# Two multi-head attentions whose first projections are made one stage earlier

## What is computed

```python
def multi_head(x, ctx, Wq, Wk, Wv, Wo, key_bias, bq, bk, bv, bo):   # x is normed
    q, k, v = heads(x @ Wq + bq), heads(ctx @ Wk + bk), heads(ctx @ Wv + bv)
    scores = einsum('bhqd,bhkd->bhqk', q, k) / 4 + key_bias[:, None, None, :]
    return merge(einsum('bhqk,bhkd->bhqd', softmax(scores), v)) @ Wo + bo
# layer 1 has key_bias and no bq, bk, bv, bo; layer 3 has these and no key_bias
x = x + tanh(g_xattn[n]) * attention_n(layernorm(x), ctx)
x = x + tanh(g_ffn[n]) * feed_forward_n(layernorm(x))
```

## Time and profile before

| | |
|---|---|
| median of three executions | 1390.92 us |
| the profiled execution: its own time, its span | 1390.4 us, 1388.7 us |
| busy in the span: PE, DVE, POOL, ACT | 1041.1 (75%), 803.3 (58%), 597.8 (43%), 561.4 us (40%) |
| mean granted TensorE clock | 0.859 of 2.4 GHz |
| combine of layer 0, first PE instruction to the next block's | 320.13 to 404.75 us |
| norm block ahead of layer 3, first DVE instruction to the next block's PE | 1094.85 to 1111.79 us |

### The profile page before, as it was taken

The page is one execution under the profiler, slowest core; times in us unless marked ns, Lnnn a source line. Parts: engine busy times, 40 slices in busy tenths (PEclk is TensorE's granted clock), DMA queues, the critical chain, the costliest instruction groups (busy, mean ns, idle before and its releaser), DMA issues. The chain is left out here.

```text
span 1388.7 us, 26577 instructions
## 1 busy us (share of the span) xinstructions
PE 1041.1 (75%) x8492; PEld 774.3 (56%) x8493; DVE 803.3 (58%) x1763; ACT 561.4 (40%) x1319; POOL 597.8 (43%) x746
## 2 busy tenths in 40 slices
PE   5777378884558888740799916798887689997998
PEld 3666167883336666630699912455555367776443
DVE  4666154442655877865455545455554538775876
ACT  2462023431126566533334305556552247774000
POOL 1473605565235667657000062556652247763000
PEclk9986589996669999955899966889898789997999
DMA  3463218862041111147777521000000100000000
GB/s 106 119 183 113 87 43 309 289 234 86 29 163 30 36 34 35 35 130 239 254 252 257 193 69 54 1 1 1 0 1 8 39 8 20 16 17 5 16 23 23
DMA packets 70682, 123.47 MB, mean 89 GB/s; under 512 B 15481, under 2 KB 41859, under 8 KB 70595
## 3 DMA queue, kind: packets, MB, share of 16 engines
q1 hardware_dynamic: 63011, 101.64, 22.5%
q0 software_dynamic: 7584, 20.72, 4.4%
HBM read 52.98 MB, written 24.64 MB: 56 GB/s over the span
## 5 line engine op out<-in xcount | busy, mean ns | idle before, releaser
L303 ACT ACTIVATE xnT<-bank 128x256 f32<-128x256 f32 (+1 forms) x112 | 42.2, 381 | 90.7 <-PE bank L292 89.4
L2411 PE MATMUL bank<-l0f_x_high,l_weights 128*128 128x256 bf16 x256 | 51.7, 320 | 34.0 <-issue 20.8
L2820 POOL DMA_DIRECT2D l_results<-keep x23 | 12.5, 544 | 135.3 <-DVE keep L2923 135.3
L3182 PE MATMUL bank<-l_weights,room 128*128 x552 | 65.1, 273 | 4.3 <-DVE room L3210 2.8
L3170 PE MATMUL bank<-room,xnT 128*128 128x128 bf16 x1104 | 67.1, 222 | 0.0
L3170 PEld LDWEIGHTS bank<-room,xnT 128*128 128x128 bf16 x1104 | 65.3, 99 | 0.3
L882 PE MATMUL bank<-ident,l_weights 128*77 128x128 f32 x256 | 39.7, 298 | 33.0 <-DVE l_weights L1073 28.3
L2243 DVE SCALAR_TENSOR_TENSOR l3f_total<-bank,l3f_share,l3f_total 128x256 f32<-128x256 f32 x112 | 54.2, 484 | 15.6 <-PE bank L2161 11.6
L2626 PE MATMUL bank<-room,l0r_placed 128*128 128x128 bf16 x936 | 61.5, 224 | 0.0
L1783 POOL TENSOR_TENSOR l2x_probs<-l2x_probs,l2x_inverse 128x333 f32<-128x333 f32 x64 | 49.5, 796 | 25.4 <-DVE l2x_inverse L1688 25.4
L3182 PEld LDWEIGHTS bank<-l_weights,room 128*128 128x128 bf16 x552 | 52.7, 98 | 12.3 <-issue 5.4
(11 more groups left out here) (430 smaller groups left out, 3252.0 us busy)
## 6 DMA issues: line engine op xcount, KB each, us to landing
xnT<-l_weights SPq DMA_DIRECT2D x23, 1024.0 KB, 5.0
l0r_placed<-l_weights SPq DMA_DIRECT2D x39, 512.0 KB, 3.6
room<-in_L_ffn_weights SPq DMA_DIRECT2D x20, 512.0 KB, 5.0
l0w_staging<-in_L_ffn_weights SPq DMA_DIRECT2D x16, 480.0 KB, 3.8
l_weights<-in_L_ffn_weights SPq DMA_DIRECT2D x16, 384.0 KB, 3.1
room<-l_rows SPq DMA_DIRECT2D x39, 128.0 KB, 3.1
l_results<-room POOLq DMA_DIRECT2D x39, 128.0 KB, 3.1
l_rows<-l_weights SPq DMA_DIRECT2D x16, 184.0 KB, 2.2
```

What stands on the lines that cost most here:

```text
L303: act.activation(self.chip.xnT[:, :, span(t, P)], bank[:, 0:DIM].rearrange("p (k n) -> p k n", k=KD), ACT.Copy).then_inc(self.copied, 1)
L2411: last = pe.matmul(self.bank[:, c, branch * width:(branch + 1) * width], self.weights[w][:, at:at + P], x[:, s, k, :], start=(i == 1), sto ...
L3182: last = pe.matmul(bank[:, 2 + u, 0:DIM], h[:, u, c * P:(c + 1) * P], expert_part(split[:, w, :, :], e, KD * hidden_width + c * DIM, DIM), ...
```

## The change

`multi_head_loads` becomes a class `HeadsAhead`, which holds the loads, the keys and first queries (now in `chip.room`; the queries take the place of `Wk`), layer 1's bias rows, and for layer 3 the values (in `chip.keep`). Its methods are called in the block before. Keys go through banks 2 and 3, values through 4 and 5, two batches to a copy.

```diff
 class HeadsAhead(Loads):
+    def tensor_keys(self, pe, chunks=range(KD)):
+        pe.wait_ge(self.loaded, 16 * len(self.copies))
+        for m in chunks:
+            for h in range(2):
+                wait(pe, self.kT_ready, 2 * m - 1 + h)
+                ...
+    def tensor_queries(self, pe, norm):
+        pe.wait_ge(norm.copied, TPB)
+        pe.wait_ge(self.kT_ready, 2 * KD)
+        ...
+    def tensor_values(self, pe, twos):
+        for n in twos:
+            wait(pe, self.v_ready, n - 1)
+            ...
+    def vector_values(self, dve, twos):
+        for n in twos:
+            dve.wait_ge(self.v_projected, n + 1)
+            ...
 # multi_head_attention
-            project_q(0)
-            project_v(range(BATCH // 2))
+            project_v(early)       # layer 1: batches 0 to 2, layer 3: none
 ...
-            project_v(range(BATCH // 2, BATCH))
+            project_v(late)        # layer 1: batches 3 to 7, layer 3: none
 # relu_square_experts, first block, SP
+                sp.wait_ge(logits_ready, 1)
+                ahead.sync(sp)
 # relu_square_experts, last block
-                ahead.sync(sp)
-                tiles.tensor(pe)
+                ahead.tensor_keys(pe, range(1))
+                tiles.tensor(pe, range(4))
+                ahead.tensor_keys(pe, range(1, 2))
+                tiles.tensor(pe, range(4, 8))
+                ahead.tensor_values(pe, range(2))
+                tiles.tensor(pe, range(8, 12))
+                ahead.tensor_values(pe, range(2, 4))
+                ahead.tensor_queries(pe, norm)
+                tiles.tensor(pe, range(12, TILES))
 # ... DVE there, group g: moments of g, norming of g - 1, and then
+                    if g >= 2:
+                        ahead.vector_values(dve, range(2 * g - 4, 2 * g - 2) if g < tiles.groups else ())
 # combine
-            sp.wait_ge(gathered[groups - 1], 16 * per * sort.picks)
+            if not heads:
+                sp.wait_ge(gathered[groups - 1], 16 * per * sort.picks)
             ahead.sync(sp)
+            if heads:                       # DVE, ahead of group 0
+                ahead.vector_bias(dve)
+            if heads:                       # PE, ahead of its tiles; ACT likewise
+                ahead.tensor_keys(pe)
+                if g == 0 and heads:        # after group 0's tiles
+                    ahead.tensor_queries(pe, norm)
```

More of the change, by code:

```diff
@@ L785, in multi_head_attention @@
         if key_bias:
-            bias = given.bias
-            bias_parts = [st.sb(f"bias_{n}", [P, CTX], BF16) for n in ("high", "mid")]
-            bias_rows = st.sb("bias_rows", [P, CTX], BF16)
+            bias_rows = given.bias_rows
             ones = st.sb("ones", [P, P], BF16)
         else:
[L791 to L794, removed]
+            bq, bo = given.bq, given.bo
+        given.start()
+        early = range(0 if given.values_ahead else 3)
+        late = range(len(early), 0 if given.values_ahead else BATCH)
         v_projected = st.sem("v_projected")
@@ L831, in _ @@
         def _(pe):
[L832 to L838, removed]
             def project_q(b):
@@ L957, in _ @@
         def _(act):
[L958 to L963, removed]
             def copy_q(b):
-                act.wait_ge(q_projected, b + 1)
+                act.wait_ge(q_projected, b)
                 wait(act, scores_ready, GROUPS * TPB * b)
@@ L1000, in _ @@
             exponents(0, 0)
-            act.wait_ge(v_ready, BATCH)
+            if len(late):
+                act.wait_ge(v_ready, BATCH)
             act.wait_ge(ones_ready, 2)
@@ L1033, in _ @@
                 clearing.vector(dve)
+            if key_bias:
+                dve.memset(ones[:, :], 1.0).then_inc(bias_ones_ready, 1)
             dve.memset(v1[:, :, :, HEAD:HEAD + 1].rearrange("p b h d -> p (b h) d"), 1.0).then_inc(ones_ready, 1)
-            dve.wait_ge(loaded, 16 * loads)
             dve.memset(zeros[:, :], 0.0).then_inc(ones_ready, 1)
             dve.wait_ge(ones_ready, 2)
[L1038 to L1051, removed]
+            if not key_bias:
                 dve.tensor_scalar(bo[:, :], bo[:, :], chip.gate[:, gate:gate + 1], None,
-                                  ALU.mult).then_inc(bias_ready, 1)
+                                  ALU.mult).then_inc(out_bias_ready, 1)
             def copy_v(batches_of):
@@ L2095, in _ @@
             def _(dve):
-                tiles.vector(dve)
+                for g in range(tiles.groups + 1):
+                    if g < tiles.groups:
+                        norm.vector_stats(dve, *tiles.group(g))
+                    if g > 0:
+                        for t, u in tiles.group(g - 1):
+                            norm.vector_apply(dve, t, u)
+                    if g >= 2:
+                        ahead.vector_values(dve, range(2 * g - 4, 2 * g - 2) if g < tiles.groups else ())
 def nth_row(dram, i):
@@ L2939, in combine @@
         part_added = st.sem("part_added")
+        heads = isinstance(ahead, HeadsAhead)
+        if heads:
+            ahead.bias_rooms(st)
         early = 2
@@ L3010, in _ @@
                 shared.scalar(act, n, n % 2)
+            if heads:
+                ahead.scalar_keys(act)
             for g in range(groups):
@@ L3013, in _ @@
                     norm.scalar(act, t, u)
+                if g == 0 and heads:
+                    ahead.scalar_queries(act)
 def relu_experts(chip, a, weights, split_before, ahead):
@@ L3277, in attention_loads @@
     if layer < len(LAYERS):
-        return multi_head_loads(chip, a, layer)
+        return HeadsAhead(chip, a, layer)
     return Loads(chip, "none")
```

142 lines of the change are left out of this document (104 added, 38 removed).

## The result

| | changed kernel | kernel before |
|---|---|---|
| median of 19 runs each | 1394.86 us | 1388.22 us |
| lowest to highest | 1388.85 to 1398.66 | 1378.68 to 1394.15 |
| profiled execution, its span | 1390.31, 1388.6 | 1390.4, 1388.7 |
| ratio, 95% interval | 1.0052 [1.0034, 1.0071] | |

The change makes the kernel slower, by 7.2 us by the ratio, with an interval of 4.7 to 9.9 (0.3% to 0.7%). The two profiled executions hide that: the one of after is among the fastest of its 19, the one of before lies 2.2 us above its median, and their spans are 0.1 us apart. So the traces are good for stretches, not for the total.

What follows compares the result with a forecast made beforehand. It took the DVE-POOL-DVE path to bound layer 0's combine and DVE to pace the norm block. Layer 1 -1.4 and layer 3 +3.0 gave +1.6 on 1390.4, 1392.0; the median 0.5 higher, 1392.5 us (range 1387.0 to 1399.5).

Steps and rivals of the forecast that it cites:

- Bias rows: Layer 0's combine: eight bias steps now stand uncovered on DVE before the first gathered rows are added, +4.2 us.
- Keys and queries in the combine: Layer 0's combine: layer 1's keys and first queries go into idle time of PE and ACT, costing nothing.
- Scores' start: Layer 1's attention: first scores 4.5 instead of 10.98 us behind the block's start, -6.5 us (-8.3 to -5.6).
- Fifth late value: Layer 1's attention: five late values instead of four before the first turning of probabilities, +0.9 us.
- Layer 1 in sum: Layer 1's terms together: 4.2 - 6.5 + 0.9 = -1.4 us (-3.2 to +0.5).
- Norm block: Ahead of layer 3: PE's added keys, values and queries lengthen it by 11.2 us, plus 1.2 for a possible clock fall.
- Attention: Layer 3's attention: scores 3.3 instead of 12.44 us behind the start, -9.1; whole attention -9.4 us (-10.9 to -6.7).
- The rest: Layer 3's attention: ACT's high part no longer waits for late values, -1.8 us; scores starting at half clock, +1.5.
- Layer 3 in sum: Norm block and attention of layer 3 together: 11.2 + 1.2 - 9.4 = +3.0 us.
- Rival 1: Norm block and layer 1's values: clock stays at 2.4 GHz, faster, 1388.0 us; chance 0.20.
- Rival 2: Norm block ahead of layer 3: runs mostly at 1.2 GHz, slower, 1397.7 us; chance 0.20.
- Rival 3: Layer 0's combine: moved loads hold up engines beside the gathers, 0 to +6 us, taken as 5, 1397.5; chance 0.12.

## Why the prediction was right, and where not

It forecast 1392.5 us with slower and same about even; measured 1394.86, and slower. By its steps:

- *Bias rows* +4.2: +4.40, and shown by the kernel that moves them (-3.8 in stretch 1). *Keys and queries in the combine*: free, as said (the kernel that has them there, and the bias steps elsewhere, is 0.85 us longer until the attention). *Scores' start* -6.5: -5.8, since all 12 early records of values ran at half clock, where I had four at full. *Fifth late value* +0.9: +1.2. Layer 1 in sum -1.4: -0.05 in the first pair, -0.3 to -2.2 on the second chip.
- *Norm block* +11.2 and +1.2 for the clock: +11.3 in the first profile, +12.6 and +12.8 in the two others, each with the wait of PE (2.91 or 2.92) that the text had at 3 us, and with DVE's before it (3.2 to 3.6). *Attention* -9.1 until the scores: -9.1. The rest, -1.8 + 1.5: +0.5, since the first 16 scores cost 2.4 us more in that profile, and 1.5 in the second. Layer 3 in sum +3.0: +2.7 in the first pair; over all profiles 43.2 on average with it and 39.1 without, +4.1, and +1.8 with the loop behind, which the sum left out.
- *The clock*. Rival 1 (it stays up) falls: the first 16 records of scores took 7.54 us in one profile of the changed kernel and 6.63 in the other, where 5.17 is full clock. Rival 2 (the block mostly at 1.2 GHz) falls as well: PEclk was 0.87 in it.
- *Rival 3*, loads beside the gathers, falls: ACT's long wait is 14.39 us against 14.38, and the stretch before the first addition is longer by the bias steps alone.
- *What was off is the sum against the medians*: predicted +1.6, by the two stretches +2.6 in the first pair and +2.4 in the second chip's, by the ratios +7.2 (4.7 to 9.9) on the first chip and +2.7 (-0.8 to +6.2) on the second. On the first, 4.6 us are in neither of the two stretches that the change touches, and I haven't found them. Layer 1's loop, counted like the other, takes 173 to 182 us without a pattern by kernel, which can hide such a difference; layer 3's loop is no place for it, being 141 us in all three profiles with the whole part.
- *Luck in the forecast*. The 0.41 for slower came mostly from rivals 2 and 3, and both fell; the forecast's own +1.6 lies inside the 2.8 us that the prediction called no change, and below the measured interval. The forecast time, 1392.5 against 1394.86, was nearer than the forecast difference because its base, one execution and three runs, lay 2.7 us above the median of all 19.
- *A step that was incomplete*: "the norm block has only the 4.1 us before its first tile to hide it in". It has more: PE waits for DVE in each group, and 16 records beyond the first half of the keys cost 1.5 us. The 32 records of values no longer fit: of what they add to the stretch, 5.5 to 7 us are PE's own work, as it costs behind the last tile, and 3.1 to 3.7 come from standing between the tiles, by the waits of DVE and PE for each other and the clock behind them.

## What to carry to other kernels

Before work is moved beside a chain, find the engine that sets that chain's pace: what goes to the others is nearly free as long as it fits into the time for which they wait (24 records of PE for 1.5 us), and what goes beyond it costs nearly its own time (5.5 to 7 us for the 32 records of values, which take 7.07): with them PE was busy for 21.4 us in a block that had taken 15.1, more than DVE's 14.7. Work that makes the chain's engine wait in its middle costs more again, 3.1 to 3.7 us here. And ask what covers the work where it stands now: in the attention the values had cost 1.2 us of the stretch. A wait of the pacing engine is the place for work that it must do itself: eight steps of 4.2 us cost 4.4 at the head of the combine and 0.85 in DVE's wait of 3.97, and with that layer 1's part is 4.3 us under before (1.1 to 7.5), where as first placed no difference was to be seen.

## What the runs showed of the hardware

*The same program, 51 us apart on two chips.* Before took 1388 us in the first measurement, 1388.3 and 1392.3 in the two later series, and 1336.5 on what is called the second chip here, and by the two profiles 52 of the 56 us between their spans lie ahead of layer 1's attention. Beside POOL's back-to-back gathers, PE on the first chip got through 102 matmuls in 35 us, 21 of them in the last 23; on the second it made 192 in 26 us:

```profile
320.00:355.00 35.00, 18.16 (x102) 11.12 (x103) 7.03 (x16) 5.15 (x13) 23.20 (x24) 0.65 0.32 90
```

```profile
291.00:317.00 26.00, 23.92 (x192) 20.04 (x192) 16.64 (x41) 9.64 (x26) 19.09 (x20) 0.88 0.32 93
```

The gathers themselves move as much on both (90 and 93 GB/s at a share of 0.32). On the first chip PE's matmuls come one by one from 332 us on, most about 1.4 us apart, and the profile has nothing that they wait for ("issue"); ACT's wait of 14.38 us ends when that does. The second chip's trace has no such wait; the profile of before in the last series has it again (13.72 us). That it is instructions that come late is my guess; no run tests it. The Trainium skill, "Runtime: NRT & Kernel Launch", "Instruction fetch mechanics", calls the fetch mostly hidden: the second chip agrees, and the other two profiles of before would be the exceptions if the guess is right.

*Around a jump over skipped code all engines stand for 1.9 to 5.2 us.* Between the shared expert's last addition and the norm block's first instruction every engine reads a count and jumps over the routed experts. The first row of the block in the second profile of before, and in the two of the kernel with keys and queries ahead:

```profile
1036.54 1.41 DVE L199 BATCH_NORM_STATS2 l2f_ln_stats<-x_res 128x6 f32<-128x256 f32 x4 [2.23 <-PEq L2014]
```

```profile
1085.63 1.40 DVE L199 BATCH_NORM_STATS2 l2f_ln_stats<-x_res 128x6 f32<-128x256 f32 x4 [2.22 <-PEq L2532]
```

```profile
1089.49 1.41 DVE L199 BATCH_NORM_STATS2 l2f_ln_stats<-x_res 128x6 f32<-128x256 f32 x4 [4.97 <-PEq L2532]
```

In the earlier trace rows it is 5.21. Two programs show both lengths, so it is no property of the change, though in the second chip's four profiles it went with layer 3's part (2.2 and 1.9 us without, 4.7 and 4.4 with it). No program has two profiles that are known to be from one chip, so whether it changes between executions on one chip isn't shown, nor how much of it is the jump: a block's meeting without one takes PE 1.83 us in the earlier trace rows.

*The clock rises at another place in each profile.* The first 16 records of keys in layer 3's attention, at the same place of the same program, took 7.42 us in one profile of before, and in the two others:

```profile
1053.48 6.70 PE L836 MATMUL bank<-ctxT,room 128*128 128x308 f32 x16 [1.83 <-PEq L113]
```

```profile
1107.45 4.38 PE L836 MATMUL bank<-ctxT,room 128*128 128x308 f32 x16 [1.83 <-PEq L113]
```

In two kernels that have the same code there and were timed on one chip (bias steps in the gap, and layer 3's loads alone) they took 6.77 and 5.77. 16 records at full clock are 4.2 us, so the engine was at 2.4 GHz from near the start in the last, and for the last few records only in the first. The Trainium skill, "TensorE: Matmul & The Clock Gate", Part 1, says that this place depends on the phase of a monitor that runs freely; these agree. It makes stretch 3 of before vary by 3.0 us (40.2 to 37.2), as much as these records (7.42 to 4.38).
